# Two key tiles per pass of probabilities times values in a causal attention block

## Chip, cores and metric

The kernel runs on one core of one Trainium2 chip. The metric is the device time of one launch in microseconds. TensorE (PE) does the matmuls, VectorE (DVE) and ScalarE (ACT) take their results from PSUM, GpSimd (POOL) does masks and some small work, SyncE (SP) issues most DMAs.

## What is computed

A block of one sequence of 2048 tokens with 128 features: layer norm with a modulation, causal attention with 8 heads of 16 features, a residual, a second norm and a small mixture of experts. What matters here is the attention:

```
h = _layernorm(x, axis=-1) * (1 + ca) + sa
q, k, v = (h @ Wq.T, h @ Wk.T, h @ Wv.T)          # 8 heads of 16
scores = jnp.einsum('bhqd,bhkd->bhqk', q, k) / scale
scores = jnp.where(causal[None, None], scores, -inf)
probs = jax.nn.softmax(scores, axis=-1)
context = jnp.einsum('bhqk,bhkd->bhqd', probs, v)
x = x + ga * context
...
```

(`scale` is 4. The last part, norm, gate and experts, is done per query block once its context is there.)

## The kernel before

The queries are cut into five blocks (`BLOCKS`: three of 512 queries, two of 256), the heads into two halves of four: ten items `n`. For each item three kinds of work run on TensorE.

First the **maxima** (L942, L948): for each query tile of 128, and for each two heads and each chunk of up to 512 keys, two matmuls put scores in a pair of PSUM banks, and VectorE reduces them to row maxima (L710). The maxima are transposed (L1027), copied by ScalarE into `max_row` (L661), and DMAs on SyncE (L506) put them as two more rows into `q_stack`, so that the later scores come out with the maximum subtracted.

Then, for each key tile `j` of the item (a "batch" `b`, 108 in all), the **scores** (L926): keys on the partitions, queries along the row, four heads in as many slots of one bank (512-query blocks) or two slots of two heads (256-query blocks). ScalarE turns each slot into probabilities (L610) in buffer `b % 4` of `probs` (`PROB_BUFS` is 4). On the diagonal GpSimd zeroes what is masked (L583).

Then the **pass of probabilities times values** (L964): four fp32 matmuls, one for each head, each into its own 32 rows of one PSUM bank, `ctx_ps`. Each matmul leaves two records in the trace, so a pass of one tile has 8. The semaphore `pv_done` counts finished passes. ScalarE waits for pass `b - 4` before it overwrites a buffer. When the last pass of an item is done, ScalarE copies `ctx_ps` (L668), TensorE transposes it (L1033), and the next item's first pass may start.

The order of all this is not written out but planned: `plan()` keeps streams of steps (maxima, scores, passes, preparation of later tokens, finish of blocks) and puts, again and again, the step with the smallest planned start (plus a bias, 400 ns for passes) on the list. Each engine runs its part of the one list in order. Every PSUM user takes one of seven banks, maxima a pair of them. A planned pass costs its columns at 2.4 GHz plus 80 ns. The keys and queries of later tokens (512 at a time, a "group") go through DRAM: `store` (L488) and `stack` (L497) on SyncE fill `k_stack` and `q_stack`, and the maxima of a block wait for them.

Of the kernel before, what the change touches and what calls it, by code (L numbers as in the profile page):

```python
# [36 lines left out]
P = 128  # L37
# [8 lines left out]
TG = 4  # L46
# [17 lines left out]
PROB_BUFS = 4  # L64
PREPARED_AFTER = {2: 1, 3: 2}
# [74 lines left out]
def estimate(s, batches):  # L140
# [12 lines left out]
    if kind == "probs_v":  # L153
        return score_width(*batches[s[1]]) * 4 / 2.4 + 80, [], PROBS_V_PASSES
# [36 lines left out]
def plan():  # L191
# [10 lines left out]
    last_batch = {n: b for b, (n, _) in enumerate(batches)}  # L202
# [13 lines left out]
    for m, spread in zip(by_pair[1], spreads[10:12] + [("values", 0), ("values", 1)]):  # L216
# [5 lines left out]
               [("probs_v", b) for b in range(len(batches))],  # L222
# [4 lines left out]
    for n in range(NI):  # L227
        before[("max_reduce", n)] = maxima[n][-1]
        before[("max_high", n)] = ("max_reduce", n)
        before[("max_sum", n)] = ("max_high", n)  # L230
        before[("max_t", n)] = ("max_sum", n)
        before[("context", n)] = ("probs_v", last_batch[n])
        before[("context_t", n)] = ("context", n)
# [12 lines left out]
    def ready(s):  # L246

        if s[0] == "scores":
            needs = [("max_t", batches[s[1]][0])] + ([("probs_v", s[1] - PROB_BUFS)] if s[1] >= PROB_BUFS else [])
        elif s[0] == "probs_v":  # L250
            n, j = batches[s[1]]
            needs = [("scores", s[1], score_slots(n) - 1)] + ([("context", n - 1)] if n and j == 0 else [])
# [51 lines left out]
    while any(streams):  # L304
# [15 lines left out]
        if s[0] == "probs_v" and last_batch[batches[s[1]][0]] == s[1]:  # L320
            n = batches[s[1]][0]
            streams[0] += [("context", n), ("context_t", n), ("context_add", n)] + (finish(n // 2) if n % 2 else [])
# [3 lines left out]
def block_kernel(nc, x_in, wq_in, wk_in, wv_in, gate_w_in, expert_w_in, out_w_in, c_in, wmod_in, out):  # L326
    steps, banks_of, last_users = plan()
    batches = item_batches()
    last_batch = {n: b for b, (n, _) in enumerate(batches)}
# [12 lines left out]
    with ExitStack() as ctx:  # L342
# [244 lines left out]
        def _(act):  # L587
# [9 lines left out]
            for step in steps:  # L597
# [4 lines left out]
                if step[0] == "scores":  # L602
# [5 lines left out]
                    if b >= PROB_BUFS:  # L608
                        act.wait_ge(pv_done, b - PROB_BUFS + 1)
# [283 lines left out]
        def _(pe):  # L893
# [4 lines left out]
            for step in steps:  # L898
# [51 lines left out]
                elif step[0] == "probs_v":  # L950

                    b = step[1]
                    n, j = batches[b]
                    first, tiles = BLOCKS[n // 2]
                    q0, queries = first_query(b), tiles * P
                    pe.wait_ge(act_drained, act_slot[("scores", b, score_slots(n) - 1)] + 1)
                    if b in diagonal:
                        pe.wait_ge(masked, masks_until(b))
                    if j % TG == 0 and j // TG == first // TG:
                        pe.wait_ge(act_drained, act_slot[("values", j // TG)] + 1)  # L960
                    if j == 0 and n:
                        pe.wait_ge(ctx_copied, n)
                    for e in range(HALF):
                        last = pe.matmul(ctx_ps[VW * e:VW * e + VW, q0:queries], v_aug[:, j, HALF * (n % 2) + e, :],  # L964
                                         probs[:, b % PROB_BUFS, e, q0:queries], start=(j == 0),
                                         stop=(j == first + tiles - 1))
# [103 lines left out]
```

## Time and profile before

| | us |
|---|---|
| median of 3 runs | 302.49 |
| lowest, highest | 302.0, 303.42 |
| span of the profiled execution | 300.6 |
| PE busy in it | 273.2 (91%) |
| DVE busy | 214.6 (71%) |
| ACT busy | 198.0 (66%) |
| PE ctx_ps L964 in the chain that ended last | 22% |

The span goes from the first to the last instruction of one execution. "x8" is a count of records, "us" of a merged row is their time together. Idle time stands in brackets with what ended it. PEclk is the granted TensorE clock, in tenths of 2.4 GHz.

### The profile page before, as it was taken

What the parts mean: (1) busy time and instruction counts of PE and PEld (TensorE: products, weight loads), DVE (VectorE), ACT (ScalarE), POOL (GpSimd) and SP (SyncE); (2) the same over time, 40 slices, a digit from 0 to 9 for tenths busy, and PEclk for the clock granted to TensorE, in tenths of its full rate; (3) what the DMA queues carried; (4) which work ended last, traced back from release to release, by engine and by line L of the source; (5) the groups of instructions that cost most, each with busy time, mean ns of one, the idle gap of its engine ahead of it and who ended that gap; (6) DMA issues with size and microseconds to landing.
All of it is one profiled execution on the core that took longest, in us unless ns stands there. A gap on an engine that the chain in (4) does not pass through costs nothing.

```text
span 300.6 us, 5682 instructions
## 1 busy us (share of the span) xinstructions
PE 273.2 (91%) x2043; PEld 124.5 (41%) x2043; DVE 214.6 (71%) x413; ACT 198.0 (66%) x409; POOL 50.5 (17%) x83
## 2 busy tenths in 40 slices
PE   7999965997799999999999999999999998998943
PEld 2555631433335444434334433334445544444412
DVE  3867772899998999989988997889998702031033
ACT  2476473480377878658776686776677698988920
POOL 6953021050030320110010200020011002010020
PEclk9799995999999999999999999999999999999995
DMA  7105693029830049900000010000000100000000
GB/s 205 39 9 149 64 113 33 0 91 129 98 34 2 2 143 125 120 4 0 2 1 3 0 35 2 1 4 0 2 1 2 35 4 2 0 20 1 2 0 19
DMA packets 14094, 11.25 MB, mean 37 GB/s; under 512 B 1290, under 2 KB 13922, under 8 KB 14066
## 3 DMA queue, kind: packets, MB, share of 16 engines
q1 hardware_dynamic: 13490, 10.36, 22.0%
q10 hardware_dynamic: 576, 0.53, 0.5%
q8 instruction: 16, 0.26, 0.4%
q14 instruction: 12, 0.10, 0.1%
HBM read 7.34 MB, written 3.41 MB: 36 GB/s over the span
## 4 chain that ended last, share of the span: by engine, by line
PE 70%; DVE 8%; DMA 5%; ACT 4%; issue 3%; SPq 2%; POOL 0%; POOLq 0%; ACTq 0%; DVEq 0%
PE ctx_ps L964 22%; PE ps L926 19%; PE ps L942 17%; DVE part_max L710 6%; DMA k_stack<-piece_scratch 5%; PE ps L1044 2%; PE ps L979 2%; PE ps L948 2%; ACT probs L610 2%; SPq L497 2%; PE ps L1013 1%; PE ps L1039 1%; PE ps L1008 1%; PE ps L1033 1%; ACT h_t L675 1%
## 5 line engine op out<-in xcount | busy, mean ns | idle before, releaser
L610 ACT ACTIVATE probs<-ps 128x512 f32<-128x512 f32 (+3 forms) x312 | 153.4, 546 | 53.1 <-PE ps L926 49.9
L710 DVE TENSOR_REDUCE part_max<-ps 128x2 f32<-128x1024 f32 (+3 forms) x160 | 163.4, 1058 | 22.0 <-PE ps L942 16.0
L942 PE MATMUL ps<-k_stack,q_stack 112*128 112x512 bf16 (+3 forms) x320 | 85.0, 352 | 10.2 <-DMA k_stack<-piece_scratch 5.5
L926 PE MATMUL ps<-q_stack,k_stack 114*128 114x256 bf16 (+3 forms) x432 | 91.6, 303 | 0.6 <-ACT h_t L675 0.2
L964 PE MATMUL ctx_ps<-probs,v_aug 128*32 128x256 f32 (+3 forms) x864 | 79.9, 449 | 0.4 <-POOL probs L583 0.3
L926 PEld LDWEIGHTS ps<-q_stack,k_stack 114*128 114x128 bf16 x432 | 36.4, 98 | 56.2 <-ACT probs L610 33.8
L583 POOL TENSOR_SCALAR_AFFINE_SELECT probs<-probs 128x512 f32<-128x512 f32 x32 | 20.3, 638 | 166.0 <-ACT probs L610 165.9
L942 PEld LDWEIGHTS ps<-k_stack,q_stack 112*128 112x128 bf16 x320 | 26.8, 99 | 46.7 <-DVE part_max L710 17.6
L964 PEld LDWEIGHTS ctx_ps<-probs,v_aug 128*32 128x32 f32 x864 | 18.0, 108 | 27.6 <-ACT probs L610 16.4
L823 DVE RECIPROCAL sum_inv<-ps 128x16 f32<-128x16 f32 (+1 forms) x10 | 2.3, 229 | 34.8 <-PE ps L1033 34.8
L536 POOL TENSOR_TENSOR rstd<-var_eps,half_neg 128x4 f32<-128x4 f32 (+1 forms) x9 | 8.5, 949 | 67.2 <-DVE var_eps L736 67.2
L948 PE MATMUL ps<-mask,ident_bf 128*128 128x128 bf16 x128 | 17.9, 221 | 0.0
L948 PEld LDWEIGHTS ps<-mask,ident_bf 128*128 128x128 bf16 x128 | 12.0, 99 | 6.3
L979 PE MATMUL ps<-piece,spread 128*112 128x512 bf16 x48 | 12.1, 381 | 0.0
L661 ACT COPY max_row<-ps 8x512 bf16<-8x512 bf16 (+1 forms) x10 | 4.9, 486 | 7.1 <-PE ps L1027 6.9
L1008 PE MATMUL ps<-ident,normed 128*128 128x128 f32 x32 | 6.1, 310 | 3.7 <-DVE normed L748 3.7
L720 DVE BATCH_NORM_STATS2 bn<-x_sb 128x6 f32<-128x128 f32 x32 | 7.0, 276 | 3.3 <-DMA x_sb<-in_L_attn_hidden_states 3.2
L972 PE MATMUL ctx_ps<-zeros 128*128 128x512 bf16 x22 | 8.2, 526 | 1.3 <-DVE zeros L700 1.3
L630 ACT ACTIVATE normed<-x_sb,norm_shift,rstd 128x128 f32<-128x128 f32 x22 | 9.1, 487 | 0.0
L785 DVE TENSOR_TENSOR left<-ps,piece 128x512 f32<-128x512 f32 x8 | 5.5, 690 | 4.7 <-PE ps L1013 2.9
L1044 PE MATMUL ps<-ffn_w,h_t 128*128 128x256 f32 x32 | 8.8, 418 | 0.0
L1013 PE MATMUL ps<-h_t,w_t 128*128 128x512 f32 x16 | 8.6, 639 | 0.3 <-ACT h_t L642 0.2
(93 smaller groups left out, 166.2 us busy)
## 6 DMA issues: line engine op xcount, KB each, us to landing
q_stack<-piece_scratch SPq DMA_DIRECT2D x21, 128.0 KB, 5.8
k_stack<-piece_scratch SPq DMA_DIRECT2D x21, 128.0 KB, 6.2
piece_scratch<-piece SPq DMA_DIRECT2D x9, 256.0 KB, 2.3
x_sb<-in_L_attn_hidden_states SPq DMA_DIRECT2D x4, 256.0 KB, 4.7
out_x<-result SPq DMA_DIRECT2D x3, 256.0 KB, 2.3
wmod<-in_L_wmod ACTq DMA_DIRECT2D x1, 384.0 KB, 4.3
out_x<-result SPq DMA_DIRECT2D x2, 128.0 KB, 2.0
q_stack<-max_row SPq DMA_DIRECT2D x12, 4.0 KB
```

The source lines that it names most:

```text
L583: pool.affine_select(out=part, in_=part, compare_op=ALU.is_ge, fill=0.0, base=0, pattern=[[0, HALF], [1, P]], channel_multiplier=-1).then_ ...
L610: drained(act.activation(probs[:, b % PROB_BUFS, heads * e:heads * e + heads, q0:tiles * P], bank.rearrange("p (h q) -> p h q", h=heads)[: ...
L630: act.activation(normed[:, k % 2, t, :], x_sb[:, first + t, :], ACT.Identity, scale=rstd[:, k % 2, t:t + 1], bias=norm_shift[:, k % 2, t:t ...
L710: dve.tensor_reduce(part_max[:, n % 2, i, 2 * e:2 * e + 2, c], banks[:, :, 0:width], AX.X, ALU.max).then_inc(vec_drained, 1)
L926: last = pe.matmul(bank[:, m * tiles * P + q0:(m + 1) * tiles * P], k_stack[0:rows, h, j * P:(j + 1) * P], q_stack[0:rows, h, tile * P + q ...
L942: last = pe.matmul(banks[:, m, 0:width], q_stack[0:ROWS, h, tile * P:(tile + 1) * P], k_stack[0:ROWS, h, c * BANK:c * BANK + width], start ...
L948: last = pe.matmul(banks[:, m, width - P:width], ident_bf[:, :], mask[:, :], start=False, stop=True)
L964: last = pe.matmul(ctx_ps[VW * e:VW * e + VW, q0:queries], v_aug[:, j, HALF * (n % 2) + e, :], probs[:, b % PROB_BUFS, e, q0:queries], sta ...
L979: last = pe.matmul(bank[0:ROWS, :], spread[:, qk, m, h].rearrange("p r d -> p (r d)"), piece[m][:, qk, 0:GROUP], start=m == 0, stop=m == 2)
L1008: last = pe.transpose(bank[:, t * P:(t + 1) * P], normed[:, m % 2, t, :], ident[:, :])
L1013: last = pe.matmul(banks[:, 0, :], w_t[:, qk, :], h_t[:, g * GROUP:(g + 1) * GROUP], start=True, stop=True)
L1044: last = pe.matmul(banks[:, t // 2, (t % 2) * 2 * D:(t % 2 + 1) * 2 * D], h2_t[:, t * P:(t + 1) * P], ffn_w[:, :, :].rearrange("p e d -> p ...
```

## The change

A step `probs_v` now holds two key tiles, `PV_TILES = 2`, which always belong to one item, since every item has an even number of them. Inside it each tile keeps its own waits and its four matmuls. `pv_done` counts steps of two tiles, so ScalarE waits for step `(b - 4) // 2`, which frees two buffers at once. There are still four buffers. The planner is told the same: a pass is ready when the scores of its second tile are, and costs the columns of both plus 235 ns (two single ones cost 160).

```
+PV_TILES = 2
...
+def pass_batches(p):
+
+    return range(PV_TILES * p, PV_TILES * p + PV_TILES)
...
-        return score_width(*batches[s[1]]) * 4 / 2.4 + 80, [], PROBS_V_PASSES
+        return sum(score_width(*batches[b]) for b in pass_batches(s[1])) * 4 / 2.4 + 235, [], PROBS_V_PASSES
...
-               [("probs_v", b) for b in range(len(batches))],
+               [("probs_v", p) for p in range(len(batches) // PV_TILES)],
...
-            needs = [("max_t", batches[s[1]][0])] + ([("probs_v", s[1] - PROB_BUFS)] if s[1] >= PROB_BUFS else [])
+            needs = [("max_t", batches[s[1]][0])] + ([("probs_v", (s[1] - PROB_BUFS) // PV_TILES)] if s[1] >= PROB_BUFS else [])
...
-                        act.wait_ge(pv_done, b - PROB_BUFS + 1)
+                        act.wait_ge(pv_done, (b - PROB_BUFS) // PV_TILES + 1)
...
-                    act.wait_ge(pv_done, last_batch[n] + 1)
+                    act.wait_ge(pv_done, last_pass[n] + 1)
...
+                    for b in pass_batches(step[1]):
+                        n, j = batches[b]
+                        first, tiles = BLOCKS[n // 2]
+                        q0, queries = first_query(b), tiles * P
+                        pe.wait_ge(act_drained, act_slot[("scores", b, score_slots(n) - 1)] + 1)
+                        if b in diagonal:
+                            pe.wait_ge(masked, masks_until(b))
...
+                        for e in range(HALF):
+                            last = pe.matmul(ctx_ps[VW * e:VW * e + VW, q0:queries],
```

Since the planner's steps change, the whole list is laid out anew. Three places of TensorE's order follow. In them L926 (after: L933) are scores, L942 (L949) maxima and L948 (L955) their mask, L964 (L971) passes, L1027 (L1035) transposes of maxima, L1033 (L1041) of the context, L1008 (L1016) of the normed tokens.

The first place is on TensorE where the keys of group 1 are first needed, before the change:

```order
L926 MATMUL ps<-q_stack,k_stack 128x256 x3
L1027 MATMUL ps<-ident_bf,max_piece 8x128 x4
L964 MATMUL ctx_ps<-probs,v_aug 32x512 x4
L942 MATMUL ps<-k_stack,q_stack 128x512 x2
L926 MATMUL ps<-q_stack,k_stack 128x256
L942 MATMUL ps<-k_stack,q_stack 128x128 x2
L948 MATMUL ps<-mask,ident_bf 128x128 x2
L926 MATMUL ps<-q_stack,k_stack 128x128 x2
L964 MATMUL ctx_ps<-probs,v_aug 32x384 x4
L942 MATMUL ps<-k_stack,q_stack 128x512 x2
```

and the same place after it:

```order
L933 MATMUL ps<-q_stack,k_stack 128x256 x3
L1035 MATMUL ps<-ident_bf,max_piece 8x128 x4
L933 MATMUL ps<-q_stack,k_stack 128x256
L933 MATMUL ps<-q_stack,k_stack 128x128
L949 MATMUL ps<-k_stack,q_stack 128x512 x2
L933 MATMUL ps<-q_stack,k_stack 128x128 x3
L971 MATMUL ctx_ps<-probs,v_aug 32x512 x4
L971 MATMUL ctx_ps<-probs,v_aug 32x384 x4
L949 MATMUL ps<-k_stack,q_stack 128x128 x2
L955 MATMUL ps<-mask,ident_bf 128x128 x2
L949 MATMUL ps<-k_stack,q_stack 128x512 x2
```

The first pass stood ahead of the first maxima that wait for the load; now it stands behind them together with the second, between the first and the second maxima tile.

The second place is on TensorE in item 5, with 512 queries, before:

```order
L964 MATMUL ctx_ps<-probs,v_aug 32x512 x4
L926 MATMUL ps<-q_stack,k_stack 128x512
L942 MATMUL ps<-k_stack,q_stack 128x512 x2
L926 MATMUL ps<-q_stack,k_stack 128x512
L942 MATMUL ps<-k_stack,q_stack 128x256 x2
L948 MATMUL ps<-mask,ident_bf 128x128 x2
L926 MATMUL ps<-q_stack,k_stack 128x512 x2
L964 MATMUL ctx_ps<-probs,v_aug 32x512 x4
L942 MATMUL ps<-k_stack,q_stack 128x512 x2
```

and after:

```order
L949 MATMUL ps<-k_stack,q_stack 128x512 x2
L933 MATMUL ps<-q_stack,k_stack 128x512 x2
L949 MATMUL ps<-k_stack,q_stack 128x256 x2
L955 MATMUL ps<-mask,ident_bf 128x128 x2
L933 MATMUL ps<-q_stack,k_stack 128x512 x2
L949 MATMUL ps<-k_stack,q_stack 128x512 x2
L933 MATMUL ps<-q_stack,k_stack 128x512
L949 MATMUL ps<-k_stack,q_stack 128x512 x2
L933 MATMUL ps<-q_stack,k_stack 128x512 x2
L971 MATMUL ctx_ps<-probs,v_aug 32x512 x8
L949 MATMUL ps<-k_stack,q_stack 128x512 x2
```

A pass stood behind two or three maxima tiles; now a pass of double length stands behind a longer run of maxima and scores.

The third place is on TensorE in the tail, where no maxima are left, from the end of item 8 to item 9, before:

```order
L926 MATMUL ps<-q_stack,k_stack 128x256 x6
L964 MATMUL ctx_ps<-probs,v_aug 32x256 x4
L926 MATMUL ps<-q_stack,k_stack 128x256 x2
L964 MATMUL ctx_ps<-probs,v_aug 32x128 x4
L926 MATMUL ps<-q_stack,k_stack 128x256 x8
L1033 MATMUL ps<-ident,ctx_t 128x128 x2
L964 MATMUL ctx_ps<-probs,v_aug 32x256 x8
L926 MATMUL ps<-q_stack,k_stack 128x256 x4
L964 MATMUL ctx_ps<-probs,v_aug 32x256 x4
L926 MATMUL ps<-q_stack,k_stack 128x256 x4
```

and after:

```order
L971 MATMUL ctx_ps<-probs,v_aug 32x256 x8
L933 MATMUL ps<-q_stack,k_stack 128x128 x2
L933 MATMUL ps<-q_stack,k_stack 128x256 x8
L971 MATMUL ctx_ps<-probs,v_aug 32x256 x4
L971 MATMUL ctx_ps<-probs,v_aug 32x128 x4
L933 MATMUL ps<-q_stack,k_stack 128x256 x2
L1041 MATMUL ps<-ident,ctx_t 128x128 x2
L933 MATMUL ps<-q_stack,k_stack 128x256 x4
L971 MATMUL ctx_ps<-probs,v_aug 32x256 x8
L933 MATMUL ps<-q_stack,k_stack 128x256 x8
L971 MATMUL ctx_ps<-probs,v_aug 32x256 x8
```

One pass of a tile alternated with the four scores matmuls of a tile; now a pass of two tiles alternates with eight.

## Rows read from the trace of the kernel before

**Rows 1.** The page: busy shares, and busy tenths in 40 slices.

```profile
PE 273.2 (91%) x2043; PEld 124.5 (41%) x2043; DVE 214.6 (71%) x413; ACT 198.0 (66%) x409; POOL 50.5 (17%) x83
...
PE   7999965997799999999999999999999998998943
...
DVE  3867772899998999989988997889998702031033
ACT  2476473480377878658776686776677698988920
```

**Rows 2.** Busy time by stretch: PE, PEld, DVE, ACT, POOL, then granted clock, DMA.

```profile
48.00:88.00 40.00, 33.75 (x224) 14.92 (x228) 35.56 (x61) 19.89 (x47) 7.31 (x10) 0.93 0.48 67
88.00:236.00 148.00, 146.81 (x1046) 62.64 (x1039) 135.55 (x214) 107.22 (x223) 17.37 (x26) 1.00 0.15 23
236.00:288.00 52.00, 49.46 (x553) 22.76 (x552) 8.21 (x36) 45.60 (x91) 4.62 (x8) 1.00 0.03 9
288.00:301.00 13.00, 3.97 (x12) 2.60 (x12) 5.22 (x24) 1.15 (x3) 0.70 (x1) 0.66 0.04 11
```

**Rows 3.** Chain that ended last, in the tail: start, us, engine and line.

```profile
236.38 1.00 PE ctx_ps L964 x16
237.38 0.54 PE ps L926 x4
237.92 0.57 PE ctx_ps L964 x8
...
250.05 0.99 PE ps L926 x8
```

**Rows 4.** The same chain in the middle stage.

```profile
181.71 0.54 PE ps L942 x2
...
182.47 0.43 PE ps L942 x2
...
184.33 0.32 PE ps L926
```

**Rows 5.** Timeline of ScalarE in the tail: start, us, line, operation, count.

```profile
268.62 3.10 ACT L610 ACTIVATE probs<-ps 128x512 f32<-128x512 f32 x6 [0.35 <-PE ps L926]
...
273.90 12.79 ACT L610 ACTIVATE probs<-ps 128x512 f32<-128x512 f32 x24 [0.92 <-PE ps L926]
```

**Rows 6.** VectorE's waits from 88 to 236 us: total us, times, longest.

```profile
DVE part_max L710 <- PE ps L942: 8.6, 20, 0.9
```

**Rows 7.** Timeline around one pass of 512 queries.

```profile
185.37 0.28 PE L948 MATMUL ps<-mask,ident_bf 128*128 128x128 bf16 x2
...
186.01 1.07 PE L964 MATMUL ctx_ps<-probs,v_aug 128*32 128x512 f32 x8
187.00 0.11 PEld L942 LDWEIGHTS ps<-k_stack,q_stack 112*128 112x128 bf16 x2 [0.84 <-DVE part_max L710]
187.00 0.60 PE L942 MATMUL ps<-k_stack,q_stack 112*128 112x512 bf16 x2
...
187.65 2.36 DVE L710 TENSOR_REDUCE part_max<-ps 128x2 f32<-128x1024 f32 x2 [0.70 <-PE ps L942]
```

**Rows 8.** Timeline at the first maxima of block 1.

```profile
48.81 1.01 PE L942 MATMUL ps<-k_stack,q_stack 112*128 112x512 bf16 x2 [4.86 <-DMA k_stack<-piece_scratch]
...
50.60 1.51 PE L964 MATMUL ctx_ps<-probs,v_aug 128*32 128x384 f32 x8
...
53.11 4.42 DVE L710 TENSOR_REDUCE part_max<-ps 128x2 f32<-128x1024 f32 x5 [1.70 <-PE ps L942]
```

**Rows 9.** Timeline at the first maxima of block 2.

```profile
85.89 2.32 DVE L710 TENSOR_REDUCE part_max<-ps 128x2 f32<-128x1024 f32 x2
...
87.11 0.59 PE L942 MATMUL ps<-k_stack,q_stack 112*128 112x512 bf16 x2 [0.66 <-DMA k_stack<-piece_scratch]
```

**Rows 10.** Timeline at the last passes.

```profile
285.13 0.64 PE L964 MATMUL ctx_ps<-probs,v_aug 128*32 128x256 f32 x8
...
286.17 1.22 POOL L583 TENSOR_SCALAR_AFFINE_SELECT probs<-probs 128x512 f32<-128x512 f32 x2 [17.20 <-ACT probs L610]
...
286.95 1.01 PE L964 MATMUL ctx_ps<-probs,v_aug 128*32 128x256 f32 x16 [0.28 <-POOL probs L583]
```

More of the change, by code:

```diff
@@ L201, in plan @@
     maxima = [maxima_units(n) for n in range(NI)]
-    last_batch = {n: b for b, (n, _) in enumerate(batches)}
+    last_pass = {n: b // PV_TILES for b, (n, _) in enumerate(batches)}
     fixed = [("warm", WARM[0]), ("spread_zeros",)] + token_stats("stats", 0)
@@ L231, in plan @@
         before[("max_t", n)] = ("max_sum", n)
-        before[("context", n)] = ("probs_v", last_batch[n])
+        before[("context", n)] = ("probs_v", last_pass[n])
         before[("context_t", n)] = ("context", n)
@@ L248, in ready @@
         if s[0] == "scores":
-            needs = [("max_t", batches[s[1]][0])] + ([("probs_v", s[1] - PROB_BUFS)] if s[1] >= PROB_BUFS else [])
+            needs = [("max_t", batches[s[1]][0])] + ([("probs_v", (s[1] - PROB_BUFS) // PV_TILES)] if s[1] >= PROB_BUFS else [])
         elif s[0] == "probs_v":
-            n, j = batches[s[1]]
-            needs = [("scores", s[1], score_slots(n) - 1)] + ([("context", n - 1)] if n and j == 0 else [])
+            b = pass_batches(s[1])[-1]
+            n, j = batches[b]
+            needs = [("scores", b, score_slots(n) - 1)] + ([("context", n - 1)] if n and j < PV_TILES else [])
         elif s[0] == "maxima":
@@ L319, in plan @@
         place(s, start, used)
-        if s[0] == "probs_v" and last_batch[batches[s[1]][0]] == s[1]:
-            n = batches[s[1]][0]
+        if s[0] == "probs_v" and last_pass[batches[PV_TILES * s[1]][0]] == s[1]:
+            n = batches[PV_TILES * s[1]][0]
             streams[0] += [("context", n), ("context_t", n), ("context_add", n)] + (finish(n // 2) if n % 2 else [])
@@ L328, in block_kernel @@
     batches = item_batches()
-    last_batch = {n: b for b, (n, _) in enumerate(batches)}
+    last_pass = {n: b // PV_TILES for b, (n, _) in enumerate(batches)}
     act_slot = {s: k for k, s in enumerate([s for s in steps if s[0] in ACT_STAGES])}
@@ L950, in _ @@
                 elif step[0] == "probs_v":
[L952 to L966, printed above, removed]
+                    for b in pass_batches(step[1]):
+                        n, j = batches[b]
+                        first, tiles = BLOCKS[n // 2]
[3 more added lines that the diff above has]
+                            pe.wait_ge(masked, masks_until(b))
+                        if j % TG == 0 and j // TG == first // TG:
+                            pe.wait_ge(act_drained, act_slot[("values", j // TG)] + 1)
+                        if j == 0 and n:
+                            pe.wait_ge(ctx_copied, n)
+                        for e in range(HALF):
+                            last = pe.matmul(ctx_ps[VW * e:VW * e + VW, q0:queries],
+                                             v_aug[:, j, HALF * (n % 2) + e, :],
+                                             probs[:, b % PROB_BUFS, e, q0:queries], start=(j == 0),
+                                             stop=(j == first + tiles - 1))
                     filled = pv_done
```

## Prediction, made before the changed kernel was run

> **What bounds the kernel now.** I first read the busy shares and the slices of the page [rows 1]. TensorE is busy for 91% of the span and VectorE for 71%, but the slices tell more: TensorE stands at 9 tenths through most of them, VectorE stands at 8 or 9 from about slice 8 to slice 31, and ScalarE takes its place at the end. So I cut the span into stages [rows 2]. From 48 to 88 us VectorE does 35.56 of 40 us and TensorE 33.75: the row maxima bound it. From 88 to 236 us TensorE does 146.81 of 148 us at full clock, with VectorE close behind at 135.55. From 236 to 288 us, where no maxima are left, TensorE does 49.46 of 52 us and ScalarE 45.60. The last 13 us are a chain of small steps that the change doesn't touch. What a TensorE saving is worth is therefore: nothing before 88 us, at most the slack of VectorE up to 236 us, at most the slack of ScalarE up to 288 us.
>
> **What the change removes.** It removes neither a matmul nor a byte. What it removes are changes between two kinds of work on TensorE. In the chain of the tail [rows 3], a pass of one tile of 256 queries (8 records) takes 0.57 us, but two passes that happen to be neighbours (16 records) take 1.00, not 1.14: 0.14 less. The four scores matmuls behind a pass take 0.54, but eight behind a pass take 0.99, so the second four cost 0.45: a pass makes its follower about 0.09 to 0.11 dearer. The middle shows the same step with other followers [rows 4]: two maxima matmuls of 512 columns take 0.54 behind a pass and 0.43 elsewhere. So an alternation costs 0.23 to 0.25 us, whatever its width. By pairs in the tail: 2 x (0.57 + 0.54) = 2.22 us now, 1.00 + 0.99 = 1.99 then, 0.23 less.
>
> The step list counts the alternations. Before there are 108 passes in 98 separate places (nine places already hold two or three). After there are 54 passes in 53 places. 45 alternations go: 4 in the stage before 88 us (8 places to 4), 24 in the middle (51 to 27), 17 in the tail (39 to 22). On TensorE that is 4 x 0.24 = 1.0, 24 x 0.24 = 5.8 and 17 x 0.23 = 3.9 us.
>
> The Trainium skill has a rule for this (TensorEngine Tiling (Array Packing), Key Properties): a change of tiling mode drains the engine. TensorE: Matmul & The Clock Gate, Step-by-step, puts a drain at about 128 cycles, which at 2.4 GHz is an estimated 53 ns, 107 ns for the way in and out. By that figure the middle and the tail would give 41 x 0.107 = 4.4 us of TensorE and not 9.7. The rows measure the whole step at more than twice that, and they decide.
>
> **Tail, 236 to 288 us.** The pair costs TensorE 1.99 us. ScalarE does four exponentials of 512 elements for it: six in a row took 3.10 us, 0.517 each, and 24 in a row 12.79 us, 0.533 each, partly paced by TensorE [rows 5]. Four cost 2.07 us by the first row, so ScalarE becomes the later one by a hair, and 2.22 - 2.07 = 0.15 of the 0.23 us per pair is left. Does the coarser release of the buffers add a stall? The wait is ScalarE's, ahead of each exponential, and what queues behind it is every later exponential and the copies of context, max_row and h2_t, for which TensorE waits in turn. ScalarE may write batch b only after the pass that holds b - 4, and hears of it only when both tiles are done. In the new order (its third piece above) four slots of scores stand between passes, and the last of the next pair stands behind the pass before. Its scores end 0.3 us after that pass (0.32 behind a pass, [rows 4]), its exponential some 0.7 us later; meanwhile TensorE has 0.99 us of scores, then the first tile of the next pass, which needs nothing new (the waits stand per tile inside the pass). So the loop closes within the 2.0 us without a stall. The bounds: 17 x 0.23 = 3.9 us if ScalarE keeps up, 17 x (2.22 - 4 x 0.533) = 1.5 us if its longest row is its true pace. I take 3.0 us, above the 2.6 that 0.15 gives, since some pairs are half as wide at the diagonal.
>
> **Middle, 88 to 236 us.** TensorE could give 5.8 us. VectorE waited 8.6 us in 20 places for maxima [rows 6], the only slack that it can return, and none of those waits is long (0.9 at most). Against it works the length of a pass: 0.99 us now with 512 queries, 0.99 + 0.86 = 1.85 with two tiles (0.86 is 0.43 times two, by the slope between 0.57 and 1.00). Around the pass at 186.08 the last maxima tile was there at 185.6 and the next at 187.6, and VectorE waited 0.70 [rows 7]. A pair stretches this gap by 0.86. The new order puts more maxima close ahead of a pass in some places, not in all. The bounds: 5.8 us of gain if every pass finds one more tile of 1.2 us queued, a loss of 3.8 us by the rival below. I take 40% of the gain, 2.3 us, as the nearest row (a gap covered but for 0.70) lies between a full and an empty queue.
>
> **Start.** Before, pass 0 ran at about 43 us while everybody waited for k_stack; the maxima then came at 48.81, and VectorE had its third tile at 53.11 after a wait of 1.70 [rows 8]. Now passes 0 and 1 stand in one piece behind the first maxima tile, since they need the scores of tile 3. The pass of 384 queries took 1.51 us there at the half clock. Both tiles cost 1.7 us for the first at that clock and about 0.7 for the second at the full one, so the second maxima tile comes at about 53.2 and the third at 53.85: 0.8 us later than now, in a stage that VectorE bounds. Bounds 0 (if the stage makes it up, as 4 alternations go there) and 2 us (if the clock is late). The new step list also moves SyncE's work: the last three pairs of stack loads of group 2 no longer stand behind its wait for the third max_row. TensorE waited only 0.66 us for them, and VectorE had its tiles the while [rows 9]: taken as 0, with 0.7 at most on the good side.
>
> **End.** Pass 105 filled the time in which the last tile was exponentiated and masked: between the end of pass 104 at 285.70 and the last matmul at 287.9 lie 2.2 us [rows 10]. Now passes 104 and 105 run ahead of the last scores; behind them come scores, exponential, mask of 0.64 and the last tile: about 0.33 + 0.4 + 0.7 + 0.4 = 1.8 us, against 1.3 from the end of pass 105 before. I take 0.4 us lost.
>
> **Sum.** 3.0 + 2.3 - 0.8 - 0.4 = 4.1 us. The profiled execution has a span of 300.6 us, 1.9 below the median of 302.49, and would have 296.5. Forecast on the median: **298.4 us**.
>
> **Rivals.** First, the full gain: both slacks suffice, 5.8 + 3.9 - 1.2 = 8.5 us, 294.0. For it: TensorE is at 99% in the middle. Against it: VectorE would have to run at 95% there. Second, no gain: the neighbours take what TensorE gives. ScalarE's pace is 0.533 (1.5 us left in the tail), the middle gives nothing, the start and end lose 1.2: 302.2. For it: 45.60 of 52 us and 135.55 of 148 us of work beside. The Trainium skill states this as a rule (TensorEngine Tiling (Array Packing), PSUM Bottleneck): tiling speeds up TensorE but not the evacuation of its results, which can become the bound. Third, slower: the longer pass starves VectorE. There are 20 pairs with 512 queries after 88 us. If VectorE waits 0.62 us at each on average (0.70 is the single gap of today, 1.56 the same one stretched, 0.3 with one more tile queued), that is 12.4 us against 8.6, and the middle grows by 3.8: 302.49 - 1.8 + 3.8 = 304.5. It turns the sign from 10.4 us, 0.52 per pass. For it: the queue of tiles is short, as seven banks hold three at most. Against it: TensorE regains speed between passes.
>
> **Chances.** Forecast with its surroundings (297 to 301): 0.47. Full gain (below 297): 0.23. No gain (301 to 304): 0.16. Slower: 0.14. About 0.5% is what a measurement tells from no change, so faster 0.70, same 0.16, slower 0.14. The range leaves out one in ten at each end: 294.0 to 304.0.
>
> **What would show it.** Two tiles in one pass at 1.00 us (256 queries) and 1.85 (512), 53 places, scores behind them unchanged: the price per alternation is right. The tail from the first pass after the last maxima to the last pass: 49 us, with ScalarE's exponentials 0.50 to 0.52 apart. In the middle, VectorE's wait for maxima: below 8.6 us says gain, above 10.4 says the third rival. The third maxima tile after the load of k_stack at 49 us: 0.8 us later. The forecast is wrong if waits of the scores for ScalarE (none on the chain now) appear in the tail, or if the middle stage keeps its 148 us.

## The result and the profile after

| | before | after |
|---|---|---|
| median of 4 runs each, us | 302.96 | 310.77 |
| lowest, highest | 302.0, 303.69 | 309.25, 312.02 |
| span of the profiled execution | 300.6 | 310.3 |

The changed kernel is slower by 2.7%: the ratio is 1.0268 with an interval of 1.0223 to 1.0314. The forecast of 298.4 us was wrong, and the time lies above its range. The profiled execution after is the slowest of its four (312.02 us), so the spans differ by 9.7 us where the medians differ by 7.8.

Lines move by 7 or 8: scores L933, maxima L949, mask L955, passes L971, VectorE's maxima L717, ScalarE's exponentials L617. The page after, for [rows 1]:

```profile
PE 276.1 (89%) x2043; PEld 131.8 (42%) x2043; DVE 213.2 (69%) x413; ACT 194.9 (63%) x409; POOL 50.6 (16%) x83
...
PE   6999955997969999999998999999999899999943
...
DVE  3657671899977889879988787968999931131033
...
PEclk9599995998679999999999999999999999999995
```

VectorE's 8s and 9s are broken by more 7s and a 6, and PEclk has a dip of 8 6 7 at slices 10 to 12 that the page before doesn't have. To see which stage pays I read from both traces when the same step runs. "Start" runs from the first maxima of item 2 (they read the keys of group 1, the first ones fetched through DRAM) to the first of item 4, "middle" from there to the last maxima of item 9, "tail" from there to the end of the last pass. Before these are 38.3, 146.1 and 54.8 us, after 43.0, 152.7 and 52.2: **4.7 lost, 6.6 lost, 2.6 gained**. Another 0.9 us lies ahead of the start, where all that differs on TensorE is that pass 0 has left; the start of that step scatters by 1.8 us between all the traces of this study. The sum is 9.6 of the 9.7 us between the spans.

The stretches after, against [rows 2] (us, PE, PEld, DVE, ACT, POOL, granted clock, DMA):

```profile
48.00:88.00 40.00, 32.61 (x202) 15.09 (x202) 32.77 (x53) 13.72 (x33) 5.49 (x7) 0.82 0.52 67
88.00:236.00 148.00, 142.79 (x982) 60.36 (x982) 126.90 (x200) 105.55 (x222) 17.36 (x26) 0.99 0.15 23
...
250.00:298.00 48.00, 44.35 (x518) 23.61 (x516) 6.49 (x32) 43.92 (x92) 4.72 (x8) 1.00 0.04 10
```

Both partners of the middle are idle more: TensorE for 5.2 of 148 us where it was 1.2, VectorE for 21 where it was 12. (After, this window takes in the end of the start; from 92.7 to 245.2 us, the middle itself, it is 5.5 and 20.2 of 152.5 us.) ScalarE does about the same work. VectorE's waits from 93 to 248 us, against the 8.6 us in 20 places of [rows 6]:

```profile
DVE part_max L717 <- PE ps L949: 13.1, 18, 2.1
...
DVE part_max L717 <- PE ps L955: 2.4, 5, 1.0
```

The first row is the one to hold against [rows 6]: 13.1 us, past the 10.4 us at which the prediction put the change of sign. With the tiles that end in a mask it is 15.5 us, where before it was 9.2. The price of an alternation came out as read. The chain in the tail (start, us, what) has the pair of passes at 1.00 and the eight scores behind it at 0.98:

```profile
274.81 0.88 PE ps L933 x8
275.69 1.00 PE ctx_ps L971 x16
276.69 1.00 PE ps L933 x8
277.69 1.00 PE ctx_ps L971 x16
```

And a wide pair, in the same chain:

```profile
93.39 1.85 PE ctx_ps L971 x16
```

The start after, for [rows 8], and the hand-over to item 2 (timeline: start, us, engine, line, operation):

```profile
49.73 1.01 PE L949 MATMUL ps<-k_stack,q_stack 112*128 112x512 bf16 x2 [5.58 <-DMA k_stack<-piece_scratch]
...
50.99 3.22 PE L971 MATMUL ctx_ps<-probs,v_aug 128*32 128x512 f32 x16
...
54.78 0.42 DVE L717 TENSOR_REDUCE part_max<-ps 128x2 f32<-128x256 f32 x1 [2.78 <-PE ps L955]
...
74.20 0.60 PE L949 MATMUL ps<-k_stack,q_stack 112*128 112x512 bf16 x2
...
76.05 0.61 PE L949 MATMUL ps<-k_stack,q_stack 112*128 112x256 bf16 x2 [1.24 <-DVE part_max L717]
...
76.66 1.49 PE L949 MATMUL ps<-k_stack,q_stack 112*128 112x512 bf16 x4
...
87.31 0.38 PE L933 MATMUL ps<-q_stack,k_stack 114*128 114x512 bf16 x1 [2.29 <-DMA q_stack<-max_row]
```

The two joined passes took 3.22 us, both at the half clock, and VectorE waited 2.78 us for its second tile. Its third came at 55.57, 5.84 us after TensorE's first maxima, where it had been 4.30 [rows 8]: 1.5 us later, not 0.8. At 76.05 TensorE had waited 1.24 us for VectorE, and the next rows run at half speed (four maxima matmuls of 512 columns in 1.49 us, while two took 0.60 just before). At 87.31 the scores of item 2 wait 2.29 us for the DMA of `max_row`; before, no such wait was there. The granted clock was 0.50 from 76 to 82 us and again from 90 to 92, behind that wait; before, it was 1.00 from 74 to 92.

### The profile page after: what moved, and what is told of

Same layout as the page of the kernel before. It is cut to its first block, busy times and chain, and to the rows that moved or that the text cites. A ratio compares the mean times of both kernels' runs of the same rounds, so it can differ in the third digit from the quotient of the medians.

```text
span 310.3 us, 5684 instructions
## 1 busy us (share of the span) xinstructions
PE 276.1 (89%) x2043; PEld 131.8 (42%) x2043; DVE 213.2 (69%) x413; ACT 194.9 (63%) x409; POOL 50.6 (16%) x83
## 4 chain that ended last, share of the span: by engine, by line
PE 59%; DVE 22%; issue 6%; ACT 5%; DMA 5%; SPq 2%; POOL 0%; POOLq 0%; ACTq 0%; DVEq 0%
PE ctx_ps L971 17%; DVE part_max L717 17%; PE ps L949 13%; PE ps L933 13%; ACT probs L617 4%; PE ps L1021 3%; PE ps L987 3%; DMA k_stack<-piece_scratch 3%; PE ps L1052 2%; PE ps L1047 1%; PE ps L955 1%; DMA gate_w<-in_L_ffn_gate_W 1%; PE ps L1016 1%; DVE result L890 1%; PE ctx_ps L980 1%
## 5 line engine op out<-in xcount | busy, mean ns | idle before, releaser
L617 ACT ACTIVATE probs<-ps 128x512 f32<-128x512 f32 (+3 forms) x312 | 150.0, 546 | 63.7 <-PE ps L933 60.9
L717 DVE TENSOR_REDUCE part_max<-ps 128x2 f32<-128x1024 f32 (+3 forms) x160 | 163.0, 1058 | 31.1 <-PE ps L949 20.2
L949 PE MATMUL ps<-k_stack,q_stack 112*128 112x512 bf16 (+3 forms) x320 | 87.1, 362 | 13.0 <-DMA k_stack<-piece_scratch 5.6
L933 PE MATMUL ps<-q_stack,k_stack 114*128 114x256 bf16 (+3 forms) x432 | 89.7, 305 | 5.0 <-DMA q_stack<-max_row 2.3
L971 PE MATMUL ctx_ps<-probs,v_aug 128*32 128x256 f32 (+3 forms) x864 | 71.3, 448 | 0.6 <-ACT probs L617 0.6
L933 PEld LDWEIGHTS ps<-q_stack,k_stack 114*128 114x128 bf16 x432 | 37.6, 98 | 49.2 <-ACT probs L617 24.4
L949 PEld LDWEIGHTS ps<-k_stack,q_stack 112*128 112x128 bf16 x320 | 25.6, 100 | 52.9 <-DVE part_max L717 27.4
L971 PEld LDWEIGHTS ctx_ps<-probs,v_aug 128*32 128x32 f32 x864 | 22.7, 110 | 31.6 <-issue 14.6
L955 PE MATMUL ps<-mask,ident_bf 128*128 128x128 bf16 x128 | 18.4, 226 | 0.0
L955 PEld LDWEIGHTS ps<-mask,ident_bf 128*128 128x128 bf16 x128 | 12.4, 102 | 7.0 <-issue 0.9
L660 ACT COPY v_aug<-ps 128x512 f32<-128x512 f32 x4 | 2.3, 586 | 12.0 <-PE ps L1027 12.0
L582 POOL TENSOR_TENSOR piece<-left,piece 128x512 bf16<-128x512 f32 x6 | 6.9, 1159 | 17.8 <-ACT piece L644 17.8
L1016 PE MATMUL ps<-ident,normed 128*128 128x128 f32 x32 | 6.0, 310 | 4.3 <-DVE normed L755 3.4
```

The source lines that it names most:

```text
L617: drained(act.activation(probs[:, b % PROB_BUFS, heads * e:heads * e + heads, q0:tiles * P], bank.rearrange("p (h q) -> p h q", h=heads)[: ...
L717: dve.tensor_reduce(part_max[:, n % 2, i, 2 * e:2 * e + 2, c], banks[:, :, 0:width], AX.X, ALU.max).then_inc(vec_drained, 1)
L933: last = pe.matmul(bank[:, m * tiles * P + q0:(m + 1) * tiles * P], k_stack[0:rows, h, j * P:(j + 1) * P], q_stack[0:rows, h, tile * P + q ...
L949: last = pe.matmul(banks[:, m, 0:width], q_stack[0:ROWS, h, tile * P:(tile + 1) * P], k_stack[0:ROWS, h, c * BANK:c * BANK + width], start ...
L955: last = pe.matmul(banks[:, m, width - P:width], ident_bf[:, :], mask[:, :], start=False, stop=True)
L1016: last = pe.transpose(bank[:, t * P:(t + 1) * P], normed[:, m % 2, t, :], ident[:, :])
```

## The experiments

All were timed beside the kernel before on the same chip. "Re-planned" kernels use the changed planner, so the whole list is laid out anew. "Kept order" kernels take the list of the kernel before and only move passes in it. The stages are read as above; the kernel before has 38.3, 146.1 and 54.8.

| run | what | places | median us | ratio to before, interval | start, middle, tail |
|---|---|---|---|---|---|
| after | all pairs, re-planned | 53 | 310.77 | 1.0268, 1.0223 to 1.0314 | 43.0, 152.7, 52.2 |
| e1_tail | pairs of items 6 to 9, re-planned | 75 | 301.47 | 0.9954, 0.993 to 0.9979 | 37.7, 147.5, 52.2 |
| e2_mid | items 2 to 5, re-planned | 79 | 307.60 | 1.0154, 1.0114 to 1.0194 | 40.1, 150.6, 54.0 |
| e3_start | items 0 and 1, re-planned | 95 | 312.88 | 1.0298, 1.0241 to 1.0355 | 40.9, 151.0, 54.5 |
| e4_release | after, buffers freed per tile | 53 | 309.87 | 1.0237, 1.0188 to 1.0286 | 41.5, 152.7, 52.2 |
| e5_fused | all pairs, kept order | 53 | 310.17 | 1.0246, 1.0216 to 1.0277 | 39.1, 155.2, 51.7 |
| e6_fused2 | items 2 to 9, kept order | 56 | 308.90 | 1.0202, 1.0165 to 1.0239 | 38.7, 155.2, 51.7 |
| e7_fused01 | items 0 and 1, kept order | 95 | 305.01 | 1.0068, 1.0039 to 1.0097 | 40.0, 146.0, 54.8 |
| e7b_fused_tail | items 6 to 9, kept order | 75 | 300.11 | 0.9911, 0.9884 to 0.9937 | 38.1, 147.0, 51.7 |
| e8_number | single passes, planned 37.5 ns dearer | 99 | 307.56 | 1.0152, 1.0112 to 1.0192 | 38.3, 148.1, 57.1 |
| e9_fused_2_5 | items 2 to 5, kept order | 79 | 310.76 | 1.0265, 1.0227 to 1.0304 | 38.7, 154.3, 54.8 |
| e10_late_2_5 | e9 with a maxima tile between the halves | 98 | 309.98 | 1.0230, 1.020 to 1.026 | 38.0, 153.0, 54.7 |
| e12_early_joined | items 2 to 5, joined in the first one's place | 79 | 311.73 | 1.0292, 1.0259 to 1.0325 | 39.0, 154.2, 54.8 |
| e13_early_split | e12 with a maxima tile between | 98 | 310.35 | 1.0224, 1.0186 to 1.0262 | 39.8, 152.3, 54.7 |
| e14_shift | single passes, moved up half a distance | 99 | 315.62 | 1.0410, 1.0368 to 1.0452 | 39.7, 157.6, 54.8 |
| e15_light | before, VectorE reads half of items 4 to 9 | 98 | 301.46 | 0.9954, 0.9925 to 0.9983 | 37.4, 145.3, 54.8 |
| e16_light_joined | e9 with that half | 79 | 304.29 | 1.0046, 1.0027 to 1.0066 | 37.9, 147.9, 54.8 |

**Which items?** The first set of kernels gives each item its own number of tiles per pass (`PV_TILES` became a list; a pass of one tile is planned with the old 80 ns):

```
-PV_TILES = 2
+ITEM_TILES = [1] * 6 + [2] * 4                # e1_tail
+ITEM_TILES = [1] * 2 + [2] * 4 + [1] * 4      # e2_mid
+ITEM_TILES = [2] * 2 + [1] * 8                # e3_start
```

> Pairs of key tiles only in items 6 to 9 (256 queries), single tiles before. 75 places of passes against 98 before and 53 after. Theory 1 (the price of an alternation is real, and the loss sits in the stages with maxima and 512 queries): start and middle keep their lengths, the tail from 236 us gives what it gave in the changed kernel, about 2.5 us, ratio to before 0.990 to 0.995. Theory 2 (a coarser release of the buffers costs wherever pairs are): no gain or slower, ratio 1.00 to 1.01.

> Pairs only in items 2 to 5 (512 queries), single tiles elsewhere; 79 places of passes. Theory 1 (a pass of 1.85 us among maxima starves VectorE): the stretch from the first maxima of item 4 to the last maxima grows by about 6 us as in the changed kernel, the start does not, ratio 1.015 to 1.025. Rival (the loss of the middle is handed down from the start, by the clock and the shifted phase of the steps): the middle keeps its length, ratio 0.99 to 1.00.

> Pairs only in items 0 and 1, single tiles after them; 95 places of passes. Theory (the start loses by itself: passes 0 and 1 behind the first maxima of item 2, then the third row maxima near the scores that need them): 4 to 5 us slower, ratio 1.013 to 1.018, and the rest as before. Rival (the start makes up what it loses): ratio 1.00.

Only the narrow pairs of items 6 to 9 pay: 0.5% faster, just short of the range of the first theory, with the tail at 52.2 us as in the changed kernel. The wide pairs lose 1.5%; the middle grows by 4.5 us and not by 6, and the start, which was to stay, by 1.8. And joining the four pairs of items 0 and 1 lost 3.0%, twice what was expected, 4.9 us of it in the middle, where this kernel has single passes like the one before. So a new list can cost time by itself, joined or not.

**The release of the buffers.** e4_release keeps the changed kernel's order, and ScalarE hears of each tile:

```
-                        act.wait_ge(pv_done, (b - PROB_BUFS) // PV_TILES + 1)
+                        act.wait_ge(pv_done, b - PROB_BUFS + 1)
...
+                        if b != pass_batches(step[1])[-1]:
+                            last.then_inc(pv_done, 1)
```

> The order of the changed kernel, step by step, but the count of finished passes goes up after each tile, and ScalarE waits for its own tile again. Theory (ScalarE's wait for two tiles at once does not matter, the order and the length of the pass do): within 0.5% of the changed kernel, ratio to before 1.022 to 1.031. Rival (the coarser release is the cause): most of the 8 us comes back, ratio 0.99 to 1.005.

309.87 against 310.77, and the middle is 152.7 us in both. The coarser release isn't the cause, as the prediction had it for the tail.

**The order kept.** A function behind the planner joins the passes in the list of the kernel before. The pair stands where its second pass stood, or in 13 places just ahead of the first scores that need its buffer.

```
+def fuse(steps, batches):
+    at = {s: k for k, s in enumerate(steps)}
...
+        if n in FUSED_ITEMS and j % 2:
+            reader = at.get(("scores", b + PROB_BUFS - 1, 0), len(steps))
+            if reader < at[("probs_v", b)]:
+                early[reader] = b
```

> The order of the kernel before is kept for every step but the passes: the first pass of each pair is moved down to the second one, or both to just ahead of the first scores that need their buffers. 53 places of passes, as in the changed kernel, counted in pairs. Theory (the loss is in the order that the planner lays out anew): the start loses 1 us, the middle (first maxima of item 4 to last maxima, 146 us before, 153 in the changed kernel) gets shorter by 2 to 5 us, the tail by 3, ratio to before 0.977 to 0.990. Rival (a pass of 1.85 us starves VectorE whatever the order): the middle grows by 3 us or more, ratio 1.00 to 1.02.

> As e5_fused, but items 0 and 1 keep single passes where the kernel before has them. Theory (order): the start is that of before, the rest as in e5_fused, ratio 0.974 to 0.987 and 1 to 2 us below e5_fused if passes 0 and 1 cost what they seem to. Rival (length of the pass): 1.00 to 1.02.

> The order of before, and only the passes of items 0 and 1 in pairs (the start alone, with nothing laid out anew behind it). Theory: the stretch from the first maxima of item 2 to the first of item 4 (38.3 us before, 43.0 in the changed kernel, 40.9 in e3_start) grows by about 1 us, ratio 1.001 to 1.006, against 1.030 in e3_start, whose difference is then the order. Rival (the pass itself costs the start): 3 to 5 us and more by the clock, ratio 1.010 to 1.030.

> Single passes everywhere, as in the kernel before; only the planner's price for one is 117.5 ns above its columns (half of 235) and not 80. 110 of the 547 other TensorE steps change their place. If the order's quality is a matter of luck within some us: ratio anywhere from 0.995 to 1.02, and not 1. If the planner is robust: 1.000, within 0.3%.

With the old order the start loses only 0.8 to 1.7 us to the joined passes (e5_fused, e7_fused01). But the middle doesn't get shorter, as the theory of e5 had it; it gets worse than in the changed kernel, 155.2 us. So the pairs themselves, or their places, cost 9 us there, and in the middle the new list was the better one for pairs, by 2.5 us; what it costs is in the start (43.0 us against 39.1). e8_number shows the planner's part alone: single passes, and only the planned price of one changed from 80 to 117.5 ns, which puts 110 of the 547 other steps of TensorE in another place. It costs 1.5%.

**The tail alone, the old order:**

```
+FUSED_ITEMS = range(6, NI)
```

> The step order of the kernel before, kept word for word, only the two passes of a pair of items 6 to 9 (256 queries) are put together (98 places fall to 75). The question is whether the tail's gain stands by itself. Theory A (an alternation costs 0.23 us and the pairs of 256 queries are short enough): 23 places less give 2 to 4 us, about 299.5 to 301, ratio to before 0.988 to 0.995, tail from the last maxima to the last pass 52 us or less (before 54.8). Theory B (ScalarE's exponentials set the pace in the tail, and the maxima of items 6 to 9 suffer from the long passes as those of items 2 to 5 do): 302 to 304, ratio 0.997 to 1.004.

300.11 us, ratio 0.9911: this beats both kernels. 23 places less gave 2.5 of the 5.3 us that 23 x 0.23 makes: the tail is 3.1 us shorter, the middle 0.9 longer. The pairs of 256 queries take 1 us, as long as a single wide pass does, and most of them stand where VectorE has nothing left to do. Its stretch from 240 to 286 us has 3.7 us of idle TensorE, and ScalarE is busy for 90% of it, so the saving is near its end there:

```profile
240.00:286.00 46.00, 42.34 (x509) 23.67 (x507) 5.32 (x25) 41.34 (x88) 4.57 (x8) 1.00 0.03 7
```

**Length, lateness or spacing?** Five kernels change only where the passes of items 2 to 5 stand. Let A and B be the two of a pair and m a maxima tile. The length theory says that 1.85 us without maxima starve VectorE. Lateness says that A's buffer comes free too late. Spacing says that passes, which need none of the seven banks, must be spread evenly.

```
before   A .. s m s .. B        e9    .. m [AB]
e10      .. A m B               e12   [AB] .. m s m
e13      A m B .. s m           e14   each pass half way towards the one before
```

> The step order of the kernel before is kept, only the pairs of items 2 to 5 (512 queries) are put together, each where its second pass stood or just ahead of the first scores that need its buffer (98 places fall to 79). Theory A (a 1.85-us pass starves VectorE): nearly the whole loss of the kernel that joined items 2 to 9, about 307 to 309, ratio 1.015 to 1.02; VectorE waits 13 us or more for maxima in the middle (before 8.6). Theory B (the loss in the middle comes from items 6 and 7): 302 to 304.

> The same list as the kernel that joins the pairs of items 2 to 5, with one difference: the last maxima tile that stood ahead of each joined pass now stands between its two halves, so each is a pass of one tile again and the 98 places are back. Buffers come free equally late. It tells the length of the pass from its late place. Theory A (the 1.85-us length starves VectorE): the loss goes, 302 to 304, VectorE's waits for maxima back near 8.6 us, though TensorE spends 19 x 0.24 = 4.6 us more on alternations than the joined kernel. Theory C (the first pass stands late, its buffer comes free late, ScalarE and then TensorE wait): the loss stays or grows, 307 to 311, with ScalarE's waits in the middle near the 42 us of the joined kernels (before 32).

> The step order of the kernel before is kept but for the passes of items 2 to 5: the two of a pair are joined in the place of the FIRST one (or right behind the scores of the second tile, where those stood later). 98 places fall to 79 and no buffer comes free later than before. Theory C (lateness: the buffer of the first half comes free late, ScalarE and then TensorE wait) expects the loss to vanish and the 19 x 0.24 = 4.6 us of TensorE to show at least in part: 298 to 303 us. Theory D (spacing: a pass needs no PSUM bank and is what gives VectorE and ScalarE time to catch up; in twos, TensorE waits for banks in the long stretches between, and VectorE starves behind the pair) expects the loss to stay: 307 to 311 us, VectorE's waits for maxima in the middle 13 us or more.

> As the kernel with the pairs joined in the place of the first half, but the next maxima tile stands between the halves, so each is a pass of one tile, in 98 places. Theory C (lateness): 302 to 303.5, nothing lost and nothing gained. Theory D (spacing): 306 to 310, close to the split kernel in the late place (309.98).

> Single passes; each pass of items 2 to 5 is moved up by half its distance to the pass before it, so that the spacing stays as it was (99 places) while about as many passes are moved as in the paired kernels. Theory D (spacing): within 1.5 us of the kernel before, 301.5 to 304.5. Theory C (lateness): the same or slightly faster. Theory E (any change of the finely set order costs, whatever it is): 306 to 310.

None of the theories of length, lateness and spacing holds. e10 has passes of one tile and still loses 7 us, so length is not needed for a loss. It isn't free either: e9 loses as much although its 19 places less save 19 x 0.23 = 4.4 us of TensorE. e12 and e13 free their buffers early and lose as much as the late ones, so it isn't lateness. e14 keeps both the length and the spacing and is the slowest of all, 315.62. What remains is theory E: each of these moves away from the places of the kernel before costs. It had the sign, not the size (306 to 310). Part of e14's loss is of another kind: its passes come so early that TensorE waits 3.1 us for their own inputs (1.3 us for exponentials, 1.1 for the copy of the context, 0.7 for a mask).

What those places are for can be read in one spot that before, e9 and a later kernel share word for word but for the pass. The kernel before, timeline of TensorE:

```profile
192.36 0.61 PE L942 MATMUL ps<-k_stack,q_stack 112*128 112x512 bf16 x2
192.80 0.38 PE L926 MATMUL ps<-q_stack,k_stack 114*128 114x512 bf16 x1
193.02 0.59 PE L942 MATMUL ps<-k_stack,q_stack 112*128 112x512 bf16 x2
193.46 0.60 PE L926 MATMUL ps<-q_stack,k_stack 114*128 114x512 bf16 x2
193.98 1.06 PE L964 MATMUL ctx_ps<-probs,v_aug 128*32 128x512 f32 x8
```

and e9_fused_2_5 from the same maxima tile on, first TensorE and then VectorE:

```profile
200.38 0.60 PE L969 MATMUL ps<-k_stack,q_stack 112*128 112x512 bf16 x2
...
201.48 0.81 PE L953 MATMUL ps<-q_stack,k_stack 114*128 114x512 bf16 x3
202.31 0.61 PE L969 MATMUL ps<-k_stack,q_stack 112*128 112x512 bf16 x2
202.75 0.38 PE L953 MATMUL ps<-q_stack,k_stack 114*128 114x512 bf16 x1
203.53 0.50 PE L969 MATMUL ps<-k_stack,q_stack 112*128 112x384 bf16 x2 [0.40 <-DVE part_max L737]
...
204.40 1.92 PE L991 MATMUL ctx_ps<-probs,v_aug 128*32 128x512 f32 x16
```

```profile
201.03 1.23 DVE L737 TENSOR_REDUCE part_max<-ps 128x2 f32<-128x1024 f32 x1 [1.70 <-PE ps L969]
...
206.99 1.23 DVE L737 TENSOR_REDUCE part_max<-ps 128x2 f32<-128x1024 f32 x1 [1.37 <-PE ps L969]
```

Before, the pass fills the time in which VectorE frees a bank pair. Without it TensorE runs ahead, and at 203.53 it stands 0.40 us for VectorE. Then comes the pair, and now VectorE stands 1.37 us. Each engine waits for the other in turn. This is not the only such spot. For each place of passes between the first maxima of item 4 and the last of item 9 I took from the trace when the last signal came that the next weight load waits for. Before, at 41 of 50 places it came while the pass was running (13 times from VectorE, 28 from ScalarE). In e10 it did so at 32 of 50, in e14 at 31 of 50, in e9 at 12 of 32. The places of the kernel before hide more waits, and more for ScalarE than for VectorE. In e14 single passes are off their places just the same. After the first maxima tile of item 8 it waits for a bank of ScalarE:

```profile
204.65 0.60 PE L958 MATMUL ps<-k_stack,q_stack 112*128 112x512 bf16 x2
205.78 0.39 PE L942 MATMUL ps<-q_stack,k_stack 114*128 114x512 bf16 x1 [0.53 <-ACT probs L626]
206.10 1.06 PE L980 MATMUL ctx_ps<-probs,v_aug 128*32 128x512 f32 x8
```

The idle time understates such waits. Matmul records normally overlap by 0.16 us (192.36 + 0.61 ends behind the next start at 192.80). A wait eats the overlap first and shows as busy: in e9 the row before 202.31 ends at 202.29, so some 0.18 us are lost there and no idle time is printed. Counted by the starts of the matmuls, in the same stretch as above and beyond the shortest usual time from one start to the next, TensorE loses 6.8 us more between maxima and scores in e10 than before, while its passes cost the same. In e9 it loses 11.6 us more there, and its 18 places less save some 4 us. So the saved alternations do come out, and the waits eat them. Here are the middles of e9, e14 and the last two kernels below, 88:245, 90:250, 88:235 and 88:238:

```profile
88.00:245.00 157.00, 150.26 (x1057) 64.67 (x1055) 135.95 (x215) 105.47 (x225) 17.30 (x26) 1.00 0.15 22
```

```profile
90.00:250.00 160.00, 150.72 (x1039) 62.38 (x1036) 137.13 (x213) 105.85 (x223) 17.32 (x26) 1.00 0.14 21
```

```profile
88.00:235.00 147.00, 145.35 (x1047) 63.08 (x1046) 86.40 (x214) 107.00 (x224) 17.29 (x26) 1.00 0.16 23
```

```profile
88.00:238.00 150.00, 146.10 (x1055) 65.68 (x1047) 86.79 (x214) 104.07 (x224) 17.30 (x26) 1.00 0.16 23
```

e9 has 6.7 us of idle TensorE and e14 9.3, where [rows 2] leave 1.2. And e9's busy time is 3.5 us above that of [rows 2], in place of 4.4 below.

**Is it VectorE?** The last pair takes half of its reading away, in both orders. It leaves out part of the maxima:

```
-                    dve.tensor_reduce(part_max[...], banks[:, :, 0:width], AX.X,
+                    dve.tensor_reduce(part_max[...], banks[:, :, 0:width // 2 if n >= 4 else width], AX.X,
```

> The kernel before, but VectorE reads only the first half of the keys of each maxima tile of items 4 to 9, so that its work after 87 us falls by some 50 us (that part of the maxima is left out, everything else is done). TensorE's work and order are the same. Since TensorE is busy for 146.81 of 148 us from 88 to 236 us, all theories expect about the time before: 300 to 302.5 us. It is the base of the next run.

> The same halved reading of the maxima, with the pairs of items 2 to 5 joined in the place of the second half (79 places), the list that cost 8 us with VectorE's full work. Theory F (TensorE and VectorE couple through the banks, and the passes stood where TensorE would have waited for one) expects the loss to go and the saved alternations to show instead: 19 x 0.24 = 4.6 us for all pairs, some 3 to 4 us of them after 87 us, so 297 to 301 us, at least 1 us below the light kernel with single passes. Theory G (ScalarE's buffers and banks, or the late order itself, cost the time) expects it to stay well above the light kernel with single passes, by 3 us or more: 304 to 309.

VectorE's busy time in the middle falls from 135.55 to 86.40 us, and the kernel with single passes gains only 1.3 us: alone, VectorE costs hardly anything there. But the price of joining falls from about 8 us (310.76 against 302.57) to 2.8 (304.29 against 301.46). So some 5 of the 8 us came through VectorE. At the spot above the wait of 0.40 us is gone (timeline of e16_light_joined):

```profile
196.34 0.60 PE L969 MATMUL ps<-k_stack,q_stack 112*128 112x512 bf16 x2
196.78 0.38 PE L953 MATMUL ps<-q_stack,k_stack 114*128 114x512 bf16 x1
197.00 0.49 PE L969 MATMUL ps<-k_stack,q_stack 112*128 112x384 bf16 x2
```

Neither theory was fully right. F called for the loss to shrink, and it did, but F also expected e16 to be the faster of the two, at 297 to 301 us; 304.29 lies in the range of G. By the count above, e16 saves some 4 us at its passes and loses 5.8 us more between maxima and scores than e15, half of the 11.6. Whom TensorE waits for in this other half isn't settled. ScalarE is the candidate: TensorE's weight loads wait for its exponentials in 50 places against 35 (e16 first, then e15, 88 to 239 and 87 to 234 us), though for less time in all.

```profile
PEld ps L953 <- ACT probs L637: 16.3, 50, 0.8
```

```profile
PEld ps L926 <- ACT probs L610: 19.5, 35, 0.8
```

One more buffer of probabilities would have told. Such a kernel, e11_bufs5_2_5 (e9 with `PROB_BUFS` of 5), was written with the theory that at least half of the loss goes if buffers are what is short. It gave no time: with the fifth buffer a later tensor needs 2048 bytes of SBUF where 64 are left.

## Why the prediction was wrong, step by step

**Price of an alternation, 0.23 to 0.25 us: right.** Pair 1.00, eight scores 0.98 in the chain above. The wide pair takes 1.85 in the chain, as worked out. The Trainium skill's drain (TensorE: Matmul & The Clock Gate, Step-by-step), an estimated 107 ns for both ways, is about half of what the rows show.

**Tail, 3.0 us gained: right.** 2.6 us in the changed kernel and in e1_tail, 3.1 in e7b_fused_tail, within the bounds of 1.5 to 3.9. From the first pass after the last maxima to the end of the last it took 49.9 us, 0.9 more than the 49 named. No stall from the coarser release: right, by e4_release. ScalarE kept up: 25 exponentials in a row from 283.91 us on took 12.45 us, 0.50 each, so the 0.533 of the lower bound was not its pace. One sign was badly chosen: I had called ScalarE's exponentials absent from the chain, but before they hold 6.8% of it from 236 to 288 us (3.5 us), and after 13.2% from 247.7 to 297.6 (6.6 us), with the gain as forecast.

**Middle, 2.3 us gained: this step failed.** It lost 6.6, outside the bounds of +5.8 to -3.8. The working took a pass for something that may stand anywhere as long as VectorE's queue is full, and gave 40% of TensorE's saving by one gap of 0.70 us [rows 7]. The runs show that the place is the point. The rows had this in them. In [rows 7] VectorE was done with its tile at 186.95 (187.65 less its wait of 0.70), 0.94 us after the start of the pass, and only then could the weight load of the next maxima start, at 187.00. Without the pass TensorE would have stood for it; the pass hid the wait. I read that row for VectorE's wait behind the pass and not for TensorE's wait under it. The 0.84 us in brackets is not the size of that wait: it stands behind nearly every pass of 512 queries, also where nothing had to be waited for:

```profile
88.63 0.10 PEld L926 LDWEIGHTS ps<-q_stack,k_stack 114*128 114x128 bf16 x1 [0.84 <-issue]
```

A pass of one tile put elsewhere loses 7 to 13 us over four items (e10, e13, e14), nearly as much or more than the joined one. The length costs too: e9 and e12 are 0.8 and 1.4 us slower than their split versions, despite 19 alternations less, so it takes about 4.4 + 1 = 5 us. In the changed kernel itself the two parts can't be told apart, since its list is another.

**Start, 0.8 us lost: mis-sized, and a piece missing.** It lost 4.7, outside its bounds of 0 to 2. The joined passes alone cost 0.8 to 1.7 with the old order (e5_fused, e7_fused01); in the changed kernel both tiles ran at the half clock, 3.22 us, where I had put 2.4. The rest goes with the new list, and only e3_start and e4_release have it too: the scores of item 2 wait for the DMA of `max_row`, 2.29 us here, 1.3 in e3_start and 2.0 in e4_release. SyncE sends these rows at 83.83, behind all 14 stack loads of group 2, and the scores start 3.5 us later; before, it sent them at 76.58, between the eighth load and the ninth, and the scores started after 2.5. I had looked at this order for the loads of `k_stack` only [rows 9] and taken it as 0, with a gain at most. The clock comes on top, and it scatters: e4_release, with the same order on TensorE, took 41.5 us for the start and not 43.0, and its clock stayed up behind that wait.

**End, 0.4 us lost: about right.** From the end of the last full pass at 295.7 to the last matmul at 297.6 it takes 1.9 us, with 1.8 forecast.

**The rivals.** The slower one had the right sign, the right stage and the right sign test: VectorE's waits rose from 8.6 past 10.4 us, to 13.1. Its chance of 0.14 was too small, and its price of 3.8 us too low, since it charged only the length. None of the rivals priced that the planner lays out everything anew. e8_number shows this price by itself, 1.5% for one such list; e3_start, with four pairs joined besides, lost 3.0%. With an order that fits this tightly (TensorE idle for 1.2 of 148 us), the case "the new list is merely not as good" should have been a rival with a price and a large chance. Beside the no-gain rival stood the Trainium skill's rule that tiling speeds TensorE but not the reading of its results (TensorEngine Tiling (Array Packing), PSUM Bottleneck). e15 and e16 agree with it in part: with VectorE's reading halved, the loss falls from 8 to 2.8 us, but no gain comes out.

## What to carry to other kernels

Where two engines are both near full and coupled through a few banks, work that needs no bank is the filler, and its value is in where it stands. Before moving it, look up, for the matmul behind each piece of it, when the engine that it needs was done: if that was after the piece began, the piece hides a wait. The idle time printed for the weight load doesn't tell this, as it is about the length of the piece. When a change goes through a planner, time one kernel with only the planner's number changed and one with only the work changed in the old order; and make the change first where the neighbours are idle, here the narrow pairs of the tail (0.9% faster).

## What I had not expected

Entering and leaving the passes costs 0.23 us of TensorE, 45 such changes fewer save some 10 us of its time, and the kernel gets slower by 7.8. Moving the passes of four items up by half their distance, with nothing joined, costs 13 us (e14_shift). And from 76 to 82 us TensorE ran at the lower of its two clocks (granted clock 0.50; four maxima matmuls of 512 columns took 1.49 us, two before them 0.60), in a stretch whose granted clock fell from 0.93 [rows 2] to 0.82. It stood 1.24 us for VectorE just before. That this stall cost the clock isn't shown: e15_light, whose order there is that of the kernel before, had a granted clock of 0.60 and 0.55 from 76 to 80 us, and the kernel before had 1.00.
